# A four-layer graph network on one core: the sum pass fetches 29 of its 782 chunks row by row instead of 22, and the padding steps are no longer gathered

## What is computed

```python
edge_index = jnp.stack([src, dst])
x = x + GAT(norm(x), edge_index)        # 8 heads, softmax over the edges of a node
x = x + GCN(norm(x), src, dst)          # agg = segment_sum(x[src], dst), then a 128x128 product
x = x + PNA(norm(x), edge_index)        # mean, min, max and std over the edges of a node
x = x + GATv2(norm(x), edge_index)      # one head, softmax over the edges of a node
```

## Time and profile before

| what | value |
|---|---|
| median of three runs | 4671.6 us |
| the profiled execution's own time | 4680.27 us |
| span from its first to its last instruction | 4678.1 us |
| busy in the span: PE / DVE / ACT / POOL | 71% / 67% / 52% / 70% |
| mean granted TensorE clock | 0.743 |

### The profile page before, as it was taken

The page is one execution under the profiler, slowest core; times in us unless marked ns, Lnnn a source line. Parts: engine busy times, 40 slices in busy tenths (PEclk is TensorE's granted clock), DMA queues, the critical chain, the costliest instruction groups (busy, mean ns, idle before and its releaser), DMA issues. The chain is left out here.

```text
span 4678.1 us, 85930 instructions
## 1 busy us (share of the span) xinstructions
PE 3306.5 (71%) x21401; PEld 2868.6 (61%) x21401; DVE 3129.2 (67%) x8139; ACT 2444.3 (52%) x5474; POOL 3282.4 (70%) x3485
## 2 busy tenths in 40 slices
PE   4888888887533433344576777777796888888886
PEld 3666666666533333334566677667665777777776
DVE  5888888888533333334577777777656776666676
ACT  4766666664300000000777777777535666666665
POOL 4777777775677777776677777777524777777774
PEclk7555555555756566556899999999997888888887
DMA  7333333332122222221466666666513333333332
GB/s 139 88 88 89 87 87 88 86 88 53 50 55 56 55 56 55 56 54 41 151 188 183 182 185 187 182 186 188 148 57 79 82 82 80 82 81 80 82 81 73
DMA packets 373416, 469.23 MB, mean 100 GB/s; under 512 B 106649, under 2 KB 276655, under 8 KB 372940
## 3 DMA queue, kind: packets, MB, share of 16 engines
q0 software_dynamic: 106944, 224.90, 20.4%
q1 hardware_dynamic: 259046, 236.40, 16.9%
q10 hardware_dynamic: 6950, 2.44, 0.2%
HBM read 327.41 MB, written 134.06 MB: 99 GB/s over the span
## 5 line engine op out<-in xcount | busy, mean ns | idle before, releaser
L891 POOL DMA_INDIRECT e_G<-dr_tab,src_idx x832 | 796.6, 957 | 273.8 <-issue 236.6
L891 POOL DMA_INDIRECT v_G<-dr_tab,src_idx x832 | 794.2, 955 | 254.0 <-issue 246.4
L891 POOL DMA_INDIRECT m_G<-dr_tab,src_idx x832 | 787.1, 946 | 262.4 <-issue 210.3
L1879 POOL DMA_INDIRECT s_G<-dr_tab,chunk_src x762 | 721.0, 946 | 236.3 <-issue 225.6
L1962 PE MATMUL s_OUT<-s_G,s_S 128*128 x1664 | 374.2, 416 | 566.8 <-POOLq L1872 521.7
L1962 PEld LDWEIGHTS s_OUT<-s_G,s_S 128*128 128x128 f32 x1664 | 349.1, 320 | 591.6 <-issue 591.6
L1917 DVE TENSOR_TENSOR ACC<-ACC,s_OUT 128x129 f32 x832 | 241.2, 290 | 599.3 <-PE s_OUT L1962 489.7
L1319 PE MATMUL e_OUT<-e_RH,e_S 128*128 128x144 f32 x1664 | 511.4, 476 | 2.2 <-DVE e_RH L1205 2.2
L2189 DVE TENSOR_TENSOR ACC<-ACC,m_OUT 128x256 f32 x832 | 347.4, 418 | 236.0 <-PE m_OUT L2273 121.2
L2472 ACT COPY f_AT<-r_TP 128x512 f32<-128x512 f32 (+1 forms) x13 | 7.2, 555 | 949.8 <-PE r_TP L2494 949.8
L1319 PEld LDWEIGHTS e_OUT<-e_RH,e_S 128*128 128x128 f32 x1664 | 405.1, 327 | 35.4 <-issue 21.7
(11 more groups left out here) (381 smaller groups left out, 8169.2 us busy)
## 6 DMA issues: line engine op xcount, KB each, us to landing
dr_ends<-m_XB SPq DMA_DIRECT2D x416, 256.0 KB, 3.4
e_LR<-dr_row_loc SPq DMA_DIRECT2D x104, 256.0 KB
m_MS<-dr_row_start SPq DMA_DIRECT2D x104, 256.0 KB, 3.3
v_LR<-dr_row_loc SPq DMA_DIRECT2D x104, 256.0 KB
s_G<-dr_tab SPq DMA_DIRECT2D x1408, 0.5 KB
s_G<-dr_tab ACTq DMA_DIRECT2D x1408, 0.5 KB
e_G<-dr_tab,src_idx POOLq DMA_INDIRECT x832
m_G<-dr_tab,src_idx POOLq DMA_INDIRECT x832
```

The lines of the kernel that those rows point to most:

```text
L891: pool.indirect_dma_start(out=out, out_offset=None, in_=table, in_offset=bass.IndirectOffsetOnAxis(ap=g["src_idx"][:, step:step + 1], axis ...
L1879: pool.indirect_dma_start(out=G[:, c % (RING * GROUP), 0:D], out_offset=None, in_=table[:, :], in_offset=bass.IndirectOffsetOnAxis(ap=g["c ...
```

## The change

- The row-by-row chunks are one in six batches for each queue and not one in eight: SP takes batches 8, 14, ... 92 (15 chunks), ACT batches 12, 18, ... 90 (14 chunks).
- Chunks 782 and 783, which are padding, are no longer gathered in `sum_pass`; steps 830 and 831 no longer in the other three passes. The semaphore targets follow (`landings`).
- The node numbers in `INDEX` are shifted left by 9 (times 512) by two VectorE instructions, one in body 3 of its loop and one in body 4, each after that body's additions. They raise `index_bytes`, and SP and ACT wait for that before their first chunk.
- The rows are addressed in a view of the table as bytes, with the loaded register as the offset, and 32 registers are loaded at once instead of 8.

```diff
-SP_CHUNKS = [j * GROUP + GROUP - 1 for j in range(8, PICKS - 3, 8)]
-ACT_CHUNKS = [j * GROUP + GROUP - 1 for j in range(12, PICKS - 2, 8)]
+SP_CHUNKS = [j * GROUP + GROUP - 1 for j in range(8, PICKS - 3, 6)]
+ACT_CHUNKS = [j * GROUP + GROUP - 1 for j in range(12, PICKS - 2, 6)]
+LOADED = 32
+ROW_BYTES = 4 * D
+REAL_STEPS = CHUNKS + TILES - 1
...
 def gather_step(g, pool, table, out, step, gathered):
+    if step >= REAL_STEPS:
+        return
...
+def landings(k):
+    return 16 * (min((k + 1) * GROUP, REAL_STEPS) - k * GROUP + k // 4 * GROUP)
...
-                    dve.wait_ge(gathered[b], base[b] + 16 * GROUP * (i + 1))
+                    dve.wait_ge(gathered[b], base[b] + landings(k))
...
-            return [c for c in range(j * GROUP, (j + 1) * GROUP) if c not in SP_CHUNKS and c not in ACT_CHUNKS]
+            return [c for c in range(j * GROUP, min((j + 1) * GROUP, CHUNKS)) if c not in SP_CHUNKS and c not in ACT_CHUNKS]
...
+        table_bytes = table.bitcast(U8).rearrange("(o r) b -> o (r b)", o=1)
...
-            eng.wait_ge(index_in[q], 16 * len(by_queue[q]))
+            eng.wait_ge(index_bytes, q + 1)
...
-                for p in range(0, P, GROUP):
-                    _, nodes = nc.values_load_multi_w_load_instructions(
-                        INDEX[q][0:1, n, p:p + GROUP], engines=[kind], min_val=0, max_val=N - 1,
-                    for u, node in enumerate(nodes):
-                        eng.dma_start(G[p + u:p + u + 1, c % (RING * GROUP), 0:D], table[bass.ds(node, 1), :]).then_inc(rows_in[q][n % 2], ROW_STEP)
+                for p in range(0, P, LOADED):
+                    _, places = nc.values_load_multi_w_load_instructions(
+                        INDEX[q][0:1, n, p:p + LOADED], engines=[kind], min_val=0, max_val=(N - 1) * ROW_BYTES,
+                    for u, place in enumerate(places):
+                        eng.dma_start(G[p + u:p + u + 1, c % (RING * GROUP), 0:D].bitcast(U8), table_bytes[:, bass.ds(place, ROW_BYTES)]).then_inc(rows_in[q][n % 2], ROW_STEP)
...
                     if not (isinstance(k, int) and k == 0):
                         add(k - 1, 1 - b)
+                    if k in (3, 4):
+                        q = k - 3
+                        dve.wait_ge(index_in[q], 16 * len(by_queue[q]))
+                        V.tensor_single_scalar(INDEX[q][:], INDEX[q][:], 9, op=ALU.logical_shift_left).then_inc(index_bytes, 1)
```

More of the change, by code:

```diff
@@ L13 @@
 import math
-F32, I32, BF16 = mybir.dt.float32, mybir.dt.int32, mybir.dt.bfloat16
+F32, I32, BF16, U8 = mybir.dt.float32, mybir.dt.int32, mybir.dt.bfloat16, mybir.dt.uint8
 ALU, ACT, AX = mybir.AluOpType, mybir.ActivationFunctionType, mybir.AxisListType
@@ L1363, in gat_pass @@
         for b in range(4):
-            g["rows_gathered"][b] += 16 * GROUP * (GROUPS // 4)
+            g["rows_gathered"][b] += landings(GROUPS - 4 + b)
 def gatv2_pass(nc, g, table, minus_xr, ACC, att):
@@ L1710, in turn @@
                     if h == 0:
-                        pe.wait_ge(gathered[b], base[b] + 16 * GROUP * (i + 1))
+                        pe.wait_ge(gathered[b], base[b] + landings(k))
                     wait(pe, lz_done, 2 * (k - 1) + h + 1)
@@ L1823, in sum_pass @@
         landed = sem("landed")
+        index_bytes = sem("index_bytes")
         index_in = [sem("sp_index_in"), sem("act_index_in")]
@@ L1855, in rows_by_register @@
                     eng.wait_ge(rows_in[q][n % 2], rows_until(n - 2))
-                for p in range(0, P, GROUP):
-                    _, nodes = nc.values_load_multi_w_load_instructions(
-                        INDEX[q][0:1, n, p:p + GROUP], engines=[kind], min_val=0, max_val=N - 1,
-                        skip_runtime_bounds_check_because="the sources are numbers of nodes")
-                    for u, node in enumerate(nodes):
-                        eng.dma_start(G[p + u:p + u + 1, c % (RING * GROUP), 0:D], table[bass.ds(node, 1), :]).then_inc(rows_in[q][n % 2], ROW_STEP)
+                for p in range(0, P, LOADED):
+                    _, places = nc.values_load_multi_w_load_instructions(
+                        INDEX[q][0:1, n, p:p + LOADED], engines=[kind], min_val=0, max_val=(N - 1) * ROW_BYTES,
+                        skip_runtime_bounds_check_because="the sources are numbers of nodes, here times the bytes of a row")
+                    for u, place in enumerate(places):
+                        eng.dma_start(G[p + u:p + u + 1, c % (RING * GROUP), 0:D].bitcast(U8), table_bytes[:, bass.ds(place, ROW_BYTES)]).then_inc(rows_in[q][n % 2], ROW_STEP)
         with nc.Block() as block:
@@ L2137, in squares @@
                 def squares(k, i, b):
-                    wait_alone(act, gathered[b], base[b] + 16 * GROUP * (i + 1), stood)
+                    wait_alone(act, gathered[b], base[b] + landings(k), stood)
                     wait_alone(act, pair_done, PAIRS * (k - 1), stood)
@@ L2297, in moments_pass @@
         for b in range(Q):
-            g["rows_gathered"][b] += 16 * GROUP * (GROUPS // Q)
+            g["rows_gathered"][b] += landings(GROUPS - 4 + b)
 def gat_to_gcn(nc, g, ACC, XPA, H0):
```

## The result

The changed kernel took 4725.7 us, the median of four runs (4724.47 to 4728.57), against 4672.86 us for the kernel before on the same chip (the median of the three runs named at the start and one more): ratio 1.0115, 95% interval 1.0097 to 1.0132. It is 53 us slower; 4657 us was forecast. Its profiled execution took 4728.57 us (before: 4680.27) at a granted clock of 0.739 (0.743).

What follows compares the result with a forecast made beforehand. The prediction took the number of POOL's gathers to bound the sum pass. Sum pass -9.3, GAT -2.2 and GATv2 -2.8 made -14.3 us, from the median 4671.6 to 4657 us; own range 4651 to 4664, 8-in-10 range 4649 to 4671.

Steps and rivals of the forecast that it cites:

- POOL therefore waits for nobody in this pass: its length is the number of POOL's gathers times 1.252 us: Sum pass: 762 gathers lie over 953.0 us, one every 1.252 us, 0.947 us busy and 0.30 us issue.
- neither queue decides after its first chunk: Sum pass: SP's chunk of 50 us and ACT's of 51 us are both under the 57.6 us available.
- the slower side: Whole kernel: a time above 4680.9 us, chance 0.10, mainly from SP's queue becoming the bound.
- Nine gathers less, 11.3 us: Sum pass: POOL issues 753 gathers instead of 762, 9 x 1.252 = 11.3 us saved.
- SP and ACT keep up: Sum pass: chunks fall from 67.2 to 50 us on SP and from 67.54 to 51 us on ACT.
- rival 2: SP's loads in the sum pass: 32 registers cost as four loads of 8; chunk 56.6 us, time 4663 us; chance 0.08.
- The first chunk, 0.5 us: Sum pass: SP's first chunk ends at 1330.6 us, POOL needs it at 1331.16; 0.5 us charged, bounds 0 and 3.
- The shifts hold POOL, 1.5 us: Sum pass: VectorE's two shifts delay POOL's gathers by 0 to 3.5 us together; 1.5 us taken.
- The ends: Ends of the other passes, two gathers fewer: GAT -2.2 us, GATv2 -2.8 us, moments 0.
- Rival 1: Sum pass: multiplication stays in a register, SP's queue becomes the bound; chunk 60.6 us, time 4709 us (4691 or 4727); chance 0.09.
- Rival 3: GAT and GATv2 ends bring half, shifts hold POOL the full 3.5 us: -9.8 us, 4662 us; chance 0.15.
- gaps in POOL's gathers every 46 chunks: Sum pass: sign that the forecast is wrong because SP's queue has become the bound.

Runs made afterwards that it cites:

- the first run of the 27 chunks: Changed kernel with loads of 8, SP's shift in body 1, 15 SP chunks and 12 ACT chunks (every seven batches): 4668.4 us, ratio 0.9970.
- The padding alone: Kernel before with only the padding's gathers left out in all four passes: 4665.5 us, ratio 0.9984; on another chip 4663.7 us, ratio 0.9974.

## Why the prediction was wrong

The step that failed is the first, with the sentence "POOL therefore waits for nobody in this pass: its length is the number of POOL's gathers times 1.252 us", and with it "neither queue decides after its first chunk". It asked of the row queues only whether they would be in time, and took a gather's landing for a constant. In these runs it is one only as long as the path that the gathers share with the rows keeps up. Faster queues were priced as pure gain; what their pace does to the gathers was no term of the sum and no rival, though the slower side got its share of chance by another mechanism. From the GAT pass's last accumulation to its own, the sum pass was 54.5 us longer and not 9.3 us shorter: 69 us of stalls, 65 of them ahead of reports that waited for the gathers' own landing, less what the gathers left out give back.

Point by point:

- *Nine gathers less, 11.3 us*: the count is right, the distance 1.249 us, and where little stalls it is paid: 762 to 755 gathers shortened the sum pass from 953.0 us to 943.5 us in the first run of the 27 chunks; seven gathers are 8.8 us of that.
- *SP and ACT keep up*: right, 50.8 and 52.4 us where 50 and 51 were forecast, from two errors that cancel. A load of 32 is 2.13 us, between the 1.5 forecast and rival 2's 3.15; a row costs 0.32 us and not 0.344.
- *The first chunk, 0.5 us*: SP started 41.9 us after POOL's first gather (40.8 forecast). But its last row landed 5.7 us after its DMA and not 1.6 as before, so that POOL stood for 3.2 us at that chunk: the rows themselves were held up as the gathers were.
- *The shifts hold POOL, 1.5 us*: the gathers beside them took 1.74 and 1.24 us and not 0.94, so 1.1 us in all. The shifts themselves took 1.14 and 1.08 us where 1.8 and 1.7 were forecast: reckoned up from 896 integers, they grew less than their number. The first still ran for 0.92 us when its gather started, and lengthened it by 0.80; the second began 0.05 us after its gather.
- *The ends*: GAT -2.3 (forecast -2.2), moments -0.35 (0), GATv2 -2.4 (-2.8). The padding alone, with its gathers in the sum pass, was forecast at 7.5 us; measured 7.2 us on one chip, 12.1 on another, with intervals some 4 to 5 us either way.
- *Rival 1*: not what happened, since the multiplication is gone; its place (POOL in the report) came about through another wait, and the price was 69 us above the forecast and not 52. That its upper time, 4727 us, lies beside the measured one is chance. *Rival 3*: no.
- *What would show it wrong*: "gaps in POOL's gathers every 46 chunks" were looked for; the gaps came in runs of batches while both queues were at work, on the gathers' own landing.

Why the rows meet the gathers on one path is not shown, but a reason can be given. Each row is a single packet in the trace, so I take it to use one DMA engine. The Trainium skill, page "DMA: Bandwidth & Descriptors", section "Why a DMA increments its semaphore by 16 and not by 1", says that a transfer issued by SP or ACT that uses k of the core's 16 DMA engines uses the lowest-numbered k. By that rule every row of both queues goes through the same one of 16 engines. The trace agrees as far as it goes: one packet of a gather's 16 lags, by 2.3 to 4.0 us, and 9 rows start beside the slow packets where some 990 should. It does not name the engine of a packet, so that the path is this one engine is concluded and not shown.

## What to carry to other kernels

Before work is moved to another DMA queue, look for what the transfers share with those that set the pace: a queue can be in time and still make everybody else's transfers late. An idle line such as "DMA ... 7.3, 24" with gaps of the common length says that a landing already comes last there; what it has to spare can be worked out (here 4.2 us less 2.5). And a change of several edits is best priced, and tried, edit by edit: here the small one gave all that could be measured, and the large one had to be slowed down before it stopped costing.

## What was not expected of the hardware

- Many single-row DMAs from two queues, beside gathers every 1.25 us, are served without harm at 4.4 per us; at 4.65 the last landing of a batch comes up to 5.9 us after its last gather's start and not 3.2, and in the changed kernel's wait shown above 15 of a gather's 16 packets are on time. Between 128 and 512 bytes the number counts: such rows delay alike.
- While one of the 222 slow packets of the changed kernel is served, a row of either queue hardly ever starts (9 in 226 us).
- A register load from SBUF on SP costs by its registers: 0.784 us for 8, 1.232 for 16, 2.129 for 32, so 0.056 us for each further one, above the 0.016 to 0.041 that PE's rows suggested.
- A VectorE shift of 1.14 us on one partition, which started 0.22 us before a gather, lengthened it by 0.80 us; one of 1.08 us, which started 0.05 us after a gather, by 0.30 us.
